# Experts' stages of a four-layer transformer block: four batches in turn in scores, merges and the way back

## The chip, the cores and the metric

The kernel runs on one core of a Trainium2 chip. Its time is device microseconds of one execution. Three runs of the kernel before took 3591.03 to 3611.88 us, median 3601.45 us.

## The reference

The input x is 8 batches of 1024 tokens of 256 numbers, fp32. Four layers are added to it, each on a layer norm without weights: a banded attention, experts, a dense attention, and the same experts again. The change touches the experts alone:

```python
def _L0_ffn_ref(x, gate_w, gate_b, w1, w2):          # x is the layer norm; E = 32 experts, K = 8
    logits = jnp.einsum('bsd,ed->bse', x, gate_w) + gate_b
    probs = jax.nn.softmax(logits, axis=-2)           # over the tokens of a batch
    vals_t, idx_t = jax.lax.top_k(probs.transpose(0, 2, 1), K)   # each expert takes 8 tokens
    tok = jnp.take_along_axis(x, flat_idx[:, :, None], axis=1).reshape(b, K, E, d)
    merged = jnp.einsum('bked,bke->bed', tok, vals)   # their weighted sum
    h = jnp.einsum('bei,eih->beh', jnp.concatenate([merged, ones], -1), w1)
    h = jax.nn.gelu(h, approximate=False)
    o = jnp.einsum('bej,ejo->beo', jnp.concatenate([h, ones], -1), w2)
    out_tok = jnp.einsum('beo,bke->bkeo', o, vals)    # the same weights on the way back
    return jnp.zeros_like(x).at[jnp.arange(b)[:, None], flat_idx].add(out_tok)
...
x = x + _L0_attn_a_ref(_layernorm(x), ...)
x = x + _L0_ffn_ref(_layernorm(x, axis=-1), L0_ffn_gate_w, L0_ffn_gate_b, L0_ffn_w1, L0_ffn_w2)
x = x + _L0_attn_b_ref(_layernorm(x), ...)
x = x + _L0_ffn_ref(_layernorm(x, axis=-1), L0_ffn_gate_w, L0_ffn_gate_b, L0_ffn_w1, L0_ffn_w2)
```

## The kernel before

x stays on the chip as x_sb: 64 tiles of 128 tokens by 256 numbers, tile t being tokens 128·(t mod 8) of batch t div 8. The function ffn is called twice, as f1 and f2; both are called f_ in the profile. PSUM is taken as eight banks of 128 x 512 numbers, all under the name f_ps. Each engine runs its own list in the order in which the code writes it, and semaphores tie the lists together; no planner sets an order in this function. It has four parts.

Setup (from L1521) makes mean and 1/deviation of each tile, turns biases and gate weights, and starts to load the weights of the first four experts.

The block "choose" has three stages. In the **scores**, VectorE normalises a tile into one of four buffers (z_tile, L1654), TensorE turns it (L1593), ScalarE takes four turned tiles, a chunk, to zT (L1631), TensorE multiplies the chunk by the gate weights (logit, L1582) and VectorE adds the gate's bias (L1661). A chunk is half a batch: 512 tokens of one batch, whose 32 scores land in the 32 PSUM partitions of that batch, 32·(b mod 4). The scores of four batches stand above one another in logits, in two such groups gq. In the **choice**, for each group, VectorE finds the eight largest of a row (L1677), marks them (L1683), ScalarE makes exponentials and their sum (L1637), VectorE sets all but the marked ones to zero and divides (L1687, L1690); TensorE turns these weights wT (L1604) and ScalarE copies them to wtok (L1642). In the **merges**, the tiles are normalised anew, even ones by VectorE, odd ones by ScalarE (L1648), and TensorE sums each batch's tiles with its weights, L1615, batch after batch, into 32 partitions of a bank. The sums are copied and turned (L1697, L1621, L1702).

The block "run" first goes through the experts in groups of four (from L1781): this **loop** isn't changed. The **way back** closes it: the experts' outputs are fetched as o_batch, again four batches above one another, and for each tile TensorE multiplies a batch's 32 rows of weights by its 32 rows of outputs (L1838), two tiles to a bank, banks 6 and 7 in turn; VectorE adds the bank to x_sb (L1893). In the first experts' stage it also makes the next layer norm's statistics of each tile (L1898). In the second, each batch of eight tiles is stored when it is done, one transfer of 1 MB (L1763).

An fp32 product is two passes over the array: the trace has two MATMUL records for each matmul of the code, and one for each transpose. In rows of the profile, "128*32 128x512" is 128 rows and 32 columns of the array, and 512 columns passed through it.

## Time and profile before

| what | value |
|---|---|
| median of three runs | 3601.45 us |
| profiled execution: its time | 3609.01 us |
| profiled execution: its span | 3607.2 us |
| TensorE busy | 2978.2 us, 83% |
| VectorE busy | 1693.9 us, 47% |
| ScalarE busy | 1422.5 us, 39% |
| GpSimd busy | 756.1 us, 21% |
| mean granted clock of TensorE | 0.907 |

The two experts' stages stand at 1451 to 1777 us and at 3277 us to the end. In a table of stretches, a row has the stretch's limits and length; then, with the number of instructions in brackets, the busy time of TensorE's passes (PE), its weight loads (PEld), VectorE (DVE), ScalarE (ACT) and GpSimd (POOL); then the granted clock of TensorE as a share of 2.4 GHz, the DMA's busy share, and GB/s. A timeline's row has the start, the length from first start to last end, engine, line, operation, output and inputs, and count; in square brackets how long the engine was idle before it, and what it waited for. A pass's record covers its way through the array as well, so that passes that start 0.43 us apart are 0.59 us long; what counts for a stream of them is the distance of the starts.

### The profile page before, as it was taken

What the parts mean: (1) busy time and instruction counts of PE and PEld (TensorE: products, weight loads), DVE (VectorE), ACT (ScalarE), POOL (GpSimd) and SP (SyncE); (2) the same over time, 40 slices, a digit from 0 to 9 for tenths busy, and PEclk for the clock granted to TensorE, in tenths of its full rate; (3) what the DMA queues carried; (4) which work ended last, traced back from release to release, by engine and by line L of the source; (5) the groups of instructions that cost most, each with busy time, mean ns of one, the idle gap of its engine ahead of it and who ended that gap; (6) DMA issues with size and microseconds to landing.
All of it is one profiled execution on the core that took longest, in us unless ns stands there. A gap on an engine that the chain in (4) does not pass through costs nothing. (4 is left out here: it accounts for less than half of the span.)

```text
span 3607.2 us, 100410 instructions
## 1 busy us (share of the span) xinstructions
PE 2978.2 (83%) x45340; PEld 1688.5 (47%) x45340; DVE 1693.9 (47%) x2811; ACT 1422.5 (39%) x1390; POOL 756.1 (21%) x523
## 2 busy tenths in 40 slices
PE   0488888878788886799668999998989898997898
PEld 0255555555556565344434444444444444443345
DVE  5143444334443343610646566666665666665202
ACT  0245444444544442320015445454554555563300
POOL 0334334333433331000022111111111111110000
PEclk9788898889889887899569999999999999999896
DMA  5333333233423331269132222222222222212494
GB/s 137 83 77 89 79 88 99 60 93 78 103 75 78 82 90 26 97 273 382 15 88 54 54 54 54 54 54 54 54 54 54 54 54 54 54 19 97 167 422 163
DMA packets 233159, 344.17 MB, mean 95 GB/s; under 512 B 113306, under 2 KB 141796, under 8 KB 216356
## 3 DMA queue, kind: packets, MB, share of 16 engines
q1 hardware_dynamic: 207508, 310.01, 29.5%
q10 hardware_dynamic: 25232, 27.83, 3.3%
q8 instruction: 354, 5.80, 0.7%
q14 instruction: 65, 0.53, 0.1%
HBM read 266.15 MB, written 69.24 MB: 93 GB/s over the span
## 5 line engine op out<-in xcount | busy, mean ns | idle before, releaser
L1403 DVE TENSOR_REDUCE b_tops<-b_slot 128x8 f32<-128x1024 f32 x576 | 680.1, 1219 | 361.1 <-PE b_slot L1260 181.4
L1440 ACT ACTIVATE b_probs<-b_slot 128x1024 f32<-128x1024 f32 x576 | 583.0, 1023 | 551.4 <-PE b_slot L1260 394.7
L502 POOL COPY a_q_far<-a_q_near 96x1024 bf16<-96x1024 bf16 x128 | 259.0, 2054 | 346.1 <-PE a_slot L581 215.9
L1280 PE MATMUL b_outT_ps<-b_probs,b_v 128*17 128x128 f32 (+3 forms) x4608 | 318.0, 384 | 6.2 <-ACT b_probs L1440 5.6
L1260 PE MATMUL b_slot<-b_q_stack,b_k_stack 99*128 99x512 bf16 (+3 forms) x1280 | 274.8, 321 | 43.5 <-DVE b_tops L1403 32.8
L1207 POOL TENSOR_SCALAR_AFFINE_SELECT b_probs<-b_probs 128x1024 f32<-128x1024 f32 x128 | 139.8, 1093 | 809.1 <-ACT b_probs L1440 809.1
L870 ACT ACTIVATE a_k_far<-a_k_near 96x1024 bf16<-96x1024 bf16 x128 | 258.0, 2067 | 91.1 <-DMA a_k_near<-parts_near_dram 82.5
L1260 PE MATMUL b_slot<-b_k_stack,b_q_stack 96*128 96x512 bf16 (+3 forms) x1280 | 266.7, 323 | 29.4 <-DVE b_tops L1403 20.6
L771 DVE TENSOR_TENSOR a_probs<-a_slot,a_bias_k 128x1024 f32<-128x1024 f32 x128 | 154.1, 1217 | 188.8 <-PE a_slot L581 188.3
L780 DVE TENSOR_REDUCE a_tops<-a_slot 128x16 f32<-128x1024 f32 x128 | 156.4, 1222 | 127.4 <-PE a_slot L581 126.5
L833 ACT ACTIVATE a_probs<-a_probs 128x1024 f32<-128x1024 f32 x128 | 133.2, 1053 | 182.9 <-DVE a_probs L771 167.1
L1260 PEld LDWEIGHTS b_slot<-b_q_stack,b_k_stack 99*128 99x128 bf16 x1280 | 107.0, 99 | 204.1 <-DVE b_tops L1403 61.8
L1814 PE MATMUL f_ps<-f_w_ring,f_hidT 128*32 128x256 f32 x1024 | 184.0, 380 | 2.1 <-ACT f_hidT L1855 2.1
L1260 PEld LDWEIGHTS b_slot<-b_k_stack,b_q_stack 96*128 96x128 bf16 x1280 | 97.5, 98 | 185.4 <-DVE b_tops L1403 61.5
L621 PE MATMUL a_slot<-a_bias_q,a_ident 128*128 128x512 bf16 x256 | 102.6, 492 | 96.5 <-POOL a_q_far L502 32.9
L657 PEld LDWEIGHTS a_outT_ps<-a_probs,a_v_near 128*17 128x17 f32 x8448 | 129.6, 103 | 87.4 <-issue 76.9
L657 PE MATMUL a_outT_ps<-a_probs,a_v_near 128*17 128x64 f32 (+1 forms) x8448 | 154.5, 228 | 18.5 <-issue 13.2
L1793 PE MATMUL f_ps<-f_w_ring,f_lhs 128*32 128x512 f32 x512 | 149.8, 613 | 8.0 <-POOL f_lhs L1777 8.0
L589 PE MATMUL a_slot<-a_zT,a_wqk 128*128 128x512 f32 x256 | 147.1, 682 | 3.6 <-issue 2.1
L1880 DVE TENSOR_TENSOR f_pre<-f_ps,f_b1T 128x128 f32<-128x128 f32 x32 | 7.8, 286 | 302.9 <-PE f_ps L1802 302.9
L1280 PEld LDWEIGHTS b_outT_ps<-b_probs,b_v 128*17 128x17 f32 x4608 | 96.2, 96 | 113.2 <-issue 68.5
L799 DVE TENSOR_SCALAR a_zb<-a_slot,a_bqk 128x1024 f32<-128x1024 f32 x32 | 41.1, 1284 | 224.0 <-PE a_slot L589 183.4
(217 smaller groups left out, 4515.7 us busy)
## 6 DMA issues: line engine op xcount, KB each, us to landing
f_w_ring<-in_L_ffn_w_dram SPq DMA_DIRECT2D x128, 1024.0 KB, 9.2
parts_near_dram<-a_parts ACTq DMA_DIRECT2D x96, 256.0 KB
parts_dram<-b_parts SPq DMA_DIRECT2D x96, 256.0 KB
a_k_near<-parts_near_dram SPq DMA_DIRECT2D x128, 128.0 KB, 3.0
b_k_stack<-parts_dram SPq DMA_DIRECT2D x64, 256.0 KB, 6.8
a_q_near<-parts_near_dram SPq DMA_DIRECT2D x64, 192.0 KB, 2.9
b_q_stack<-parts_dram SPq DMA_DIRECT2D x32, 384.0 KB, 4.5
values_dram<-a_v_stage SPq DMA_DIRECT2D x16, 544.0 KB, 4.6
```

What stands on the lines that cost most here:

```text
L502: pool.tensor_copy(q_far[far][0:QK_ROWS, h, :].rearrange("p (r a) -> p r a", r=LINKS), q_near[near][0:QK_ROWS, h, :].rearrange("p (a r) -> ...
L589: return pe.matmul(dst[:, c * 512:(c + 1) * 512], wqk[:, "qk".index(kind), kd, 8 * part:8 * part + 8, :].rearrange("p h d -> p (h d)"), zT ...
L657: ins = pe.matmul(outT_ps[BLK * h:BLK * h + HD + 1, lo:top], v_near[:, c, blk % 4, (HD + 1) * h:(HD + 1) * (h + 1)], probs[h][:, at:at + t ...
L771: ins = dve.tensor_tensor(probs[h][:, :].rearrange("p (k t c) -> p k t c", k=2, c=64), src[:, :].rearrange("p (k t c) -> p k t c", k=2, c=64),
L780: ins = dve.tensor_reduce(tops[:, h, :, :].rearrange("p k t -> p (k t)"), src[:, :].rearrange("p (t c) -> p t c", c=64), AX.X, ALU.max)
L870: act.activation(k_far[far][0:QK_ROWS, h, :].rearrange("p (r a) -> p r a", r=LINKS), k_near[near][0:QK_ROWS, h, :].rearrange("p (a r) -> p ...
L1260: ins = pe.matmul(dst[:, at:at + top - lo], own[0:rows, head, P * tile:P * tile + P], other[0:rows, head, lo:top], start=True, stop=True)
L1280: ins = pe.matmul(outT_ps[32 * h:32 * h + HD + 1, first:last], v1[b % 2][:, j, HG * g + h, :], src[:, base + first:base + last], start=u = ...
L1403: ins = dve.tensor_reduce(out, src, AX.X, ALU.max)
L1440: act.activation(probs_of(b, g, u, h)[:, :], slot_of(step)[:, :], ACT.Exp).then_inc(taken_act, 1)
L1793: ins = pe.matmul(bank[n][32 * j:32 * j + 32, :], lhs1[half][:, kd, j, :], w1_ring[:, j, kd, n * 512:(n + 1) * 512], start=kd == 0, stop=k ...
L1814: ins = pe.matmul(bank[4 + half][32 * j:32 * j + 32, 0:D], hidT[half][:, c, j, :], w2_ring[:, j, c, :], start=c == 0, stop=c == HE // P - 1)
```

## The change

Tiles of four batches take turns. The function tile_at(n) gives the tile that is n-th: n mod 4 is the batch in its group, and i = (n div 4) mod 8 its place in the batch. So a chunk is now tile i of each of four batches. Four chunks fill a bank of 512 tokens for four batches.

- Scores: zb has eight buffers in place of four. logit(c) has eight products of 32x128, for kd in 2, q in 4, in place of two of 32x512. VectorE adds the bias once in four chunks, to all 128 rows. The choice of the first group is written into the scores, behind VectorE's tiles of chunks 10, 11 and 12; its exponential into ScalarE's list after chunk 11; the turned weights after the last chunk's transposes.
- Merges: tile n goes to the PSUM rows of batch q = n mod 4, bank gq. The second group's choice stands between VectorE's tiles after n = 6, 12 and 18, its exponential behind ScalarE's tile 11, its turned weights ahead of tile 32.
- Way back: a unit is two tiles of each of four batches. Eight units; 16 products in the order q = 0, 1, 2, 3 for the first tile, then for the second, each batch into a bank of its own, eight banks for two units. VectorE adds banks 0 and 1 to x_sb; ScalarE copies banks 2 and 3 to the buffer spare, and GpSimd adds spare to x_sb. VectorE makes the statistics of its own four tiles of a unit, then those of GpSimd's four of the unit before.
- Output: after each unit SP issues four transfers of two tiles (256 KB) in place of one of 1 MB for each batch.
- Some semaphores between instructions of one engine or across blocks go, with no instruction added or taken away.

The core of the diff:

```diff
-            zb = ssb("zb", [P, 4, D])
+            zb = ssb("zb", [P, 8, D])
+            def tile_at(n):
+                c, q = divmod(n, 4)
+                return (4 * (c // NT) + q) * NT + c % NT
...
                     def logit(c):
-                        b, half = c // 2, c % 2
+                        gq, i = divmod(c, NT)
                         pe.wait_ge(zT_ready, c + 1)
-                        if c >= 2:
-                            pe.wait_ge(logits_ready, c - 1)
+                        if c >= 8 and c % 4 == 0:
+                            pe.wait_ge(logits_ready, c // 4 - 1)
                         for kd in range(KD):
-                            ins = pe.matmul(bank[2 + c % 2][32 * (b % 4):32 * (b % 4) + NE, :], gate_wT[:, kd, :],
-                                            zT[:, c % 2, kd, :], start=kd == 0, stop=kd == KD - 1)
+                            for q in range(4):
+                                ins = pe.matmul(bank[2 + c // 4 % 2][32 * q:32 * q + NE, i % 4 * P:(i % 4 + 1) * P], gate_wT[:, kd, :],
+                                                zT[:, c % 2, kd, q * P:(q + 1) * P], start=kd == 0, stop=kd == KD - 1)
...
+                    for n in range(B * NT):
+                        c, q = divmod(n, 4)
+                        gq, i = divmod(c, NT)
+                        if n == 0:
+                            pe.wait_ge(wtok_ready, 2)
+                        if n == B * NT // 2:
+                            turn_weights(1)
+                            pe.wait_ge(wtok_ready, 4)
...
+                        pe.matmul(bank[gq][32 * q:32 * q + NE, 0:D], wtok[:, i, gq, 32 * q:32 * q + NE],
+                                  zb[:, n % 8, :], start=i == 0, stop=i == NT - 1).then_inc(merge_done, 1)
...
 ScalarE
+                    for n in range(1, B * NT, 2):
+                        if n < 8:
+                            act.wait_ge(z_turned, B * NT)
+                        else:
+                            act.wait_ge(merge_done, n - 7)
...
+                        if n == 11:
+                            exponentials(1)
+                        if n == B * NT // 2 - 1:
+                            take_weights(1)
...
 way back, TensorE
-                    for t2 in range(B * NT // 2):
-                        if t2 >= 2:
-                            pe.wait_ge(summed, t2 - 1)
+                    for u in range(UNITS_OUT):
+                        gq, i2 = divmod(u, NT // 2)
                         for ii in range(2):
-                            b, i = (2 * t2 + ii) // NT, (2 * t2 + ii) % NT
-                            rows = slice(32 * (b % 4), 32 * (b % 4) + NE)
-                            ins = pe.matmul(bank[6 + t2 % 2][:, ii * D:(ii + 1) * D], wT[rows, b // 4, i * P:(i + 1) * P],
-                                            o_batch[rows, b // 4, :], start=True, stop=True)
-                        ins.then_inc(scattered, 1)
+                            i = 2 * i2 + ii
+                            for q in range(4):
+                                if u >= 2 and not ii:
+                                    if q < 2:
+                                        pe.wait_ge(summed, 2 * u - 3 + q)
+                                    else:
+                                        pe.wait_ge(taken, 2 * u - 5 + q)
+                                rows = slice(32 * q, 32 * q + NE)
+                                ins = pe.matmul(bank[u % 2 * 4 + q][:, ii * D:(ii + 1) * D], wT[rows, gq, i * P:(i + 1) * P],
+                                                o_batch[rows, gq, :], start=True, stop=True)
+                                if ii:
+                                    ins.then_inc(scattered, 1)
...
 way back, GpSimd, ScalarE, SP
+                    for u in range(UNITS_OUT):
+                        for q in range(2, 4):
+                            pool.wait_ge(taken, 2 * u + q - 1)
+                            xt = two_tiles(u, q)
+                            pool.tensor_tensor(xt, spare[:, q - 2, :], xt, ALU.add).then_inc(added, 1)
...
+                            act.wait_ge(scattered, 4 * u + q + 1)
+                            if u:
+                                act.wait_ge(added, 2 * u - 3 + q)
+                            act.activation(spare[:, q - 2, :], bank[u % 2 * 4 + q][:, :], ACT.Copy).then_inc(taken, 1)
...
+                            sp.wait_ge(summed, 2 * u + 2)
+                            sp.wait_ge(added, 2 * u + 2)
...
+                                sp.dma_start(out[b, i * P:(i + 2) * P, :].rearrange("(i p) d -> p i d", p=P), x_sb[:, t:t + 2, :]).then_inc(stored, 16)
```

Three places show what the change does to the lists. The first is TensorE from the end of the scores to the end of the merges, before and after; f_zb are the normalised tiles, f_zT the turned chunk, f_wT the chosen weights.

```order
-L1582 MATMUL f_ps<-f_zT,f_gate_wT 32x512 x4
-L1604 MATMUL f_ps<-ident,f_wT 128x128 x16
-L1615 MATMUL f_ps<-f_zb,f_wtok 32x256 x64
-L1621 MATMUL f_ps<-ident,f_merged 128x128 x4
```

```order
+L1599 MATMUL f_ps<-ident,f_wT 128x128 x8
+L1590 MATMUL f_ps<-f_zT,f_gate_wT 32x128 x8
+L1629 MATMUL f_ps<-f_zb,f_wtok 32x256 x32
+L1599 MATMUL f_ps<-ident,f_wT 128x128 x8
+L1629 MATMUL f_ps<-f_zb,f_wtok 32x256 x32
+L1634 MATMUL f_ps<-ident,f_merged 128x128 x4
```

The weights of the first group are turned ahead of the last scores, and those of the second half way through the merges. The second place is VectorE from the last chunks of the scores into the merges, after the change; before, the steps MAX to the division, of both groups, stood together between the last scores and the first tile of the merges.

```order
+L1679 TENSOR_SCALAR f_zb<-x_sb,f_mv,f_rstd 128x256 x4
+L1690 MAX f_top<-f_logits 128x8
+L1692 TENSOR_SCALAR f_neg_max<-f_top 128x1
+L1679 TENSOR_SCALAR f_zb<-x_sb,f_mv,f_rstd 128x256 x4
+L1698 MATCH_REPLACE f_marked<-f_top,f_logits 128x1024
+L1679 TENSOR_SCALAR f_zb<-x_sb,f_mv,f_rstd 128x256 x4
+L1703 RECIPROCAL f_inv<-f_total 128x1
+L1704 SCALAR_TENSOR_TENSOR f_wT<-f_marked,f_wT 128x1024
+L1707 TENSOR_SCALAR f_wT<-f_wT,f_inv 128x1024
+L1679 TENSOR_SCALAR f_zb<-x_sb,f_mv,f_rstd 128x256 x4
+L1685 TENSOR_SCALAR f_logits<-f_ps,f_gate_b 128x512
```

Each step of the choice is followed by four tiles. The third is VectorE in the first way back, before and after.

```order
-L1893 TENSOR_TENSOR x_sb<-f_ps,x_sb 128x512
-L1898 BN_STATS stats<-x_sb 128x6 x2
-L1893 TENSOR_TENSOR x_sb<-f_ps,x_sb 128x512
-L1898 BN_STATS stats<-x_sb 128x6 x2
-L1893 TENSOR_TENSOR x_sb<-f_ps,x_sb 128x512
-L1898 BN_STATS stats<-x_sb 128x6 x2
```

```order
+L1976 TENSOR_TENSOR x_sb<-f_ps,x_sb 128x512 x2
+L1981 BN_STATS stats<-x_sb 128x6 x4
+L1967 BN_STATS stats<-x_sb 128x6 x4
+L1976 TENSOR_TENSOR x_sb<-f_ps,x_sb 128x512 x2
+L1981 BN_STATS stats<-x_sb 128x6 x4
+L1967 BN_STATS stats<-x_sb 128x6 x4
```

Sixteen sums of 512 numbers leave VectorE's list and stand in GpSimd's; the 64 statistics stay.

## Rows read from the trace of the kernel before

**Rows 1.** Stretches: first stage (scores, choice, merges, loop, way back), second's end

```profile
1460.20:1508.70 48.50, 47.09 (x192) 21.07 (x192) 34.10 (x81) 18.87 (x33) 0.00 (x0) 0.96 0.36 149
1508.70:1520.90 12.20, 3.94 (x16) 3.13 (x16) 9.78 (x16) 4.65 (x9) 0.00 (x0) 0.63 0.00 0
1520.90:1548.10 27.20, 27.14 (x128) 12.32 (x128) 12.37 (x30) 18.23 (x32) 0.00 (x0) 0.92 0.00 1
...
1550.60:1723.90 173.30, 161.88 (x832) 73.19 (x832) 4.63 (x18) 16.37 (x33) 4.25 (x12) 0.97 0.85 342
1723.90:1776.60 52.70, 51.05 (x128) 38.55 (x128) 45.52 (x97) 0.00 (x0) 0.00 (x0) 0.50 0.00 0
...
3550.50:3602.30 51.80, 51.06 (x128) 38.57 (x128) 22.10 (x32) 0.00 (x0) 0.00 (x0) 0.50 0.42 142
3602.30:3607.20 4.90, 0.00 (x0) 0.00 (x0) 0.02 (x1) 0.00 (x0) 0.00 (x0) 0.50 0.63 214
```

**Rows 2.** Timeline of one chunk of the first scores

```profile
1500.40 1.09 PE L1593 MATMUL f_ps<-ident,f_zb 128*128 128x128 f32 x8
1500.51 0.75 DVE L1661 TENSOR_SCALAR f_logits<-f_ps,f_gate_b 32x512 f32<-32x512 f32 x1 [0.70 <-PE f_ps L1582]
1501.15 1.09 ACT L1631 ACTIVATE f_zT<-f_ps 128x512 f32<-128x512 f32 x2 [1.77 <-PE f_ps L1593]
1501.29 1.38 DVE L1654 TENSOR_SCALAR f_zb<-x_sb,f_mv,f_rstd 128x256 f32<-128x256 f32 x4
...
1501.42 1.90 PE L1582 MATMUL f_ps<-f_zT,f_gate_wT 128*32 128x512 f32 x4
...
1503.26 1.09 PE L1593 MATMUL f_ps<-ident,f_zb 128*128 128x128 f32 x8
```

**Rows 3.** Timeline, second attention: products to four column groups

```profile
2308.44 0.41 PE L1280 MATMUL b_outT_ps<-b_probs,b_v 128*17 128x128 f32 x8
...
2321.44 1.38 PE L1280 MATMUL b_outT_ps<-b_probs,b_v 128*17 128x512 f32 x12
```

**Rows 4.** Timeline of the first stage: the exponential, ScalarE's tiles in the merges

```profile
1510.18 1.15 ACT L1637 ACTIVATE f_wT<-f_logits,f_neg_max 128x1024 f32<-128x1024 f32 x1 [3.79 <-DVE f_neg_max L1679]
...
1520.79 1.08 ACT L1648 ACTIVATE f_zb<-x_sb,f_shift,f_rstd 128x256 f32<-128x256 f32 x2
...
1522.90 0.60 ACT L1648 ACTIVATE f_zb<-x_sb,f_shift,f_rstd 128x256 f32<-128x256 f32 x1 [1.02 <-PE f_ps L1615]
```

**Rows 5.** Stretches at the start of the first scores

```profile
1460.80:1464.20 3.40, 3.39 (x16) 3.24 (x16) 3.33 (x10) 1.73 (x3) 0.00 (x0) 0.52 1.00 424
1464.20:1467.10 2.90, 2.90 (x14) 1.22 (x12) 1.53 (x4) 0.90 (x3) 0.00 (x0) 1.00 1.02 429
```

**Rows 6.** Timelines of the first way back, and of statistics before it

```profile
1730.11 1.05 PE L1838 MATMUL f_ps<-f_o_batch,f_wT 32*128 32x256 f32 x3
...
1731.26 1.05 PE L1838 MATMUL f_ps<-f_o_batch,f_wT 32*128 32x256 f32 x2
...
1730.11 0.41 PEld L1838 LDWEIGHTS f_ps<-f_o_batch,f_wT 32*128 32x128 f32 x2
...
1734.06 0.69 DVE L1893 TENSOR_TENSOR x_sb<-f_ps,x_sb 128x512 f32<-128x512 f32 x1
...
1447.97 2.70 DVE L762 BATCH_NORM_STATS2 stats<-x_sb 128x6 f32<-128x256 f32 x8
```

**Rows 7.** Lines of GpSimd's sums, and timeline of one beside VectorE

```profile
L476 POOL TENSOR_TENSOR a_spread<-a_tops,a_among x32: 664/667/676, 168.9 to 1385.5; 128x256 f32<-128x256 f32 x32
...
L488 POOL TENSOR_TENSOR a_zb<-a_zb,a_parts x32: 2119/2126/2134, 106.4 to 1292.3; 128x1024 f32<-128x1024 f32 x32
...
1298.47 4.03 POOL L494 TENSOR_TENSOR a_parts<-a_zb,a_parts 128x1024 bf16<-128x1024 f32 x1 [4.00 <-ACT a_parts L859]
...
1298.21 2.29 DVE L756 SCALAR_TENSOR_TENSOR a_flat<-a_gate,a_flat 128x2048 f32<-128x2048 f32 x1
```

**Rows 8.** A stretch inside one output transfer

```profile
3559.50:3562.00 2.50, 2.50 (x7) 2.00 (x6) 0.79 (x2) 0.00 (x0) 0.00 (x0) 0.50 1.02 348
```

218 lines of the change are left out of this document (125 added, 93 removed).

## The prediction

> **What bounds the kernel now.** I read the table of stages first, then the timeline of one step inside each stage, then the chain of waits of the last stage, and last the rows that price what the trace of before doesn't have. The two experts' stages are the only ones the change touches. In the first, scores run from 1460.2 to 1508.7, the top-8 choice to 1520.9, merges to 1548.1; then the experts' loop to 1723.9 and the way back to 1776.6 [rows 1]. The second repeats this within 0.5 us a stage (its way back, 3550.5 to 3602.3, and 4.9 us of output DMA after it are shown). The loop isn't touched: TensorE is busy in 161.88 of its 173.30 us, the DMA at 342 GB/s, and its first weights were loaded in the scores (149 GB/s over 48.5 us). So 173 us stay in each experts' stage, and what can move is 48.5 + 12.2 + 27.2 + 52.7 us in the first and the like in the second.
>
> In scores and merges TensorE is busy nearly all the time (47.09 of 48.50, 27.14 of 27.20) but each product uses 32 of the array's 128 columns. One chunk of four tiles takes 2.86 us: 1.02 us from the start of its eight transposes to the scores, 1.84 us for the scores, while VectorE works 1.38 + 0.75 us and ScalarE 1.09 us [rows 2]. In the way back each product uses 32 rows of 128, and the granted clock is 0.50, that is 1.2 GHz [rows 1].
>
> **Scores.** A chunk is now one tile of each of four batches. An fp32 product is two passes, so before it is 4 passes of 512 columns, 0.43 us apart; now it is 16 passes of 128, a quarter as long, 0.107 us, to four column groups in turn. That groups run beside each other is seen in the second attention: 8 passes of 128 columns to four groups take 0.41 us in all, where eight in series start over 0.86, and 12 of 512 columns take 1.38 us, in series 5.1 [rows 3]. So four rounds of 0.107 = 0.43, plus the 0.13 that the scores took beyond their four passes (1.84 - 1.71): 0.56, and TensorE needs 1.58 us a chunk. In series it would need 1.84 + 1.02 again: that is the other end.
>
> VectorE is then as late. Four tiles in 1.38 with 0.41 for one are 0.32 apart: 64 x 0.32 = 20.7. The bias add of four batches is one instruction of 0.75 in four chunks: 3 x 0.75 = 2.2 inside the loop. The first group's top-8 steps move into the loop: both groups together cost VectorE 9.78 us, less two tiles 8.96, so 4.5 for one. Some fifteen restarts after waits at 0.1 each make 1.5. Sum 28.9, against 16 x 1.58 + 1 (the turned weights) = 26.3 for TensorE; with eight z buffers either can be a chunk ahead, so the larger counts, not the sum. The exponential on ScalarE (1.15 us, [rows 4], and the table it loads) fits into its slack of 16 x (1.8 - 1.09). Behind the last tile stand half a transpose chunk, the turned weights, the last scores and their bias add: about 2.9. Scores: 32 instead of 48.5 us, **-16.5** (bounds: -18.5 with perfect overlap of VectorE and TensorE, 0 in series).
>
> **Top-8.** The 12.2 us in which TensorE works 3.94 go from the path: the first group's steps are in the 28.9, the second's stand between the tiles of the first merges. **-12.2** (bounds -12.2 and -7.7, if the 4.5 of the second group add to the merges).
>
> **Merges.** Before, two passes of 256 columns a tile set the pace. Now four tiles in turn go to four groups, and the next is the normalised tile itself. ScalarE makes every second one, two in 1.08 with 0.60 for one [rows 4], so 0.48 apart: 32 x 0.48 = 15.4. Into its queue come the exponential, 1.15 (all tiles behind it wait, which TensorE feels after the buffers are used up), and after tile 31 the second group's weights: TensorE turns 8 blocks, the 1.02 that eight transposes take in the scores, or double at half clock, and ScalarE copies twice: 2.3. Sum 18.9. VectorE needs 32 x 0.32 + 4.5 + hand-overs = 16, within it. 27.2 becomes 19.2: **-8** (bounds -10 and 0). For the couplings between the three engines, whose waits no row shows, I give back 2.7 in each stage: **-34** for scores to merges, -68 for both.
>
> **Way back.** 64 tiles, 128 passes of 32x256. Before all passes that follow each other are in one row group, 0.427 us apart at 1.2 GHz; only where the batch changes they overlap: three passes in 1.05 us there, two in 1.05 elsewhere, and the weight loads of two groups stand within 0.41 [rows 6]. Now four groups take turns, eight tiles a unit: 16 passes, four rounds, 1.7 us if they overlap fully, 6.8 in series. Weight loads of 128 columns come along; they overlapped at the batch change too, so I take 1.7 to 2.6. What else a unit needs: VectorE two adds, 0.69 each; ScalarE two copies, the 0.49 apart that two take in the scores (1.09 for two, [rows 2]); GpSimd two adds of 512 elements, between its 0.667 for 256 and 2.126 for 1024 [rows 7]; on the line between them 1.15, so 2.3. GpSimd's pace could suffer from VectorE: one of its adds took 4.03 us instead of 2.13 beside VectorE's operation on two SBUF inputs, 2.29 us long [rows 7]. VectorE's adds here have one input in PSUM, and its statistics one input in all, so I take no such loss; its price would be 1.4 a unit at most.
>
> First stage: VectorE also makes the statistics of eight tiles, eight in 2.70 [rows 6]; a unit is 1.4 + 2.7 + 0.1 = 4.2, longer than all others. 8 x 4.2 = 33.9, plus 2.1 until the first unit is there and 0.4 at the end: 36.4 instead of 52.7, **-16.3**. Before it was 32 x (0.69 + 0.75) = 46 of VectorE's time in the same stage, with waits; that the statistics run in blocks saves the rest.
>
> Last stage: no statistics, so the output DMA is next: eight units of 1 MB. Within a transfer the DMA moves 348 GB/s [rows 8], 3.0 us a unit, more than GpSimd's 2.3. First data after 2.1 (products) + 0.6 + 1.15 + 1.15 (copy, two adds) + 1.0 ahead of the transfer; then 24.1, and 0.9 to the end (before, 4.9 us pass from the last add to the end, of which the last 1 MB is 3.0, so 1.9 stand around it): 31.1 from the start of the way back, against 51.8 + 4.9 = 56.7: **-25.6** (bounds: -28 without any lead, 0 with row groups in series, since 8 x 6.8 = 54.4).
>
> **Sum.** -68 - 16.3 - 25.6 = -110 us. The profiled execution has a span of 3607.2 and a time of 3609.0, 0.2% over the median of the runs, 3601.45. From that median: 3491.5, so 3492.
>
> **The rivals.** *Half clock in the scores.* With the scores short, TensorE is mostly transposing, and the clock may stay at 1.2 GHz: transposes 1.7, scores 0.85 and 0.3 of hand-overs are 2.9 a chunk, no better than now. It costs 16 us a stage, 3524. Against it: in the first 3.4 us of this stage TensorE did nothing but transposes, at 0.52, and right behind the clock was 1.00 [rows 5]; and merges on a quarter of the columns are at 0.92 [rows 1]. For it: the way back stays at 0.50 with 51.05 us busy, so a busy record alone doesn't raise the clock, and the new stage leaves gaps. The Trainium skill ("TensorE: Matmul & The Clock Gate", Part 4: PE-mode transpose) says that transposes don't count as busy for the clock. By that rule this rival would be likely; the row on the 3.4 us speaks against it here.
>
> *The way back stays in series.* Weight loads of 128 columns, not the passes, set 3.4 us a unit or more, up to 6.8: the last stage gives 0 to -22, the first 0 to -16; in the middle 3512. Against it the overlap at the batch change.
>
> *The packing costs instead.* In the scores there are four times as many passes and weight loads, each pass only 0.107 long. If a load can't hide behind a pass of another column group (0.11 each, exposed), the chunk is 16 x 0.217 + 1.02 = 4.5 us: +26 a stage. If row groups behave alike, the way back gains nothing. With top-8's -12.2 and merges at 0 that is +28, 3630, slower than before. It decides where an exposed load makes the chunk longer than 2.86, so from 0.01 us a load on. The Trainium skill (the same page, Part 3: Packing small matmuls) says that loads overlap running matmuls only when the row group differs, and that matmuls start in program order. By the first half this rival would hold; the 8 passes in 0.41 us, loads included, say otherwise for column groups.
>
> **How the numbers follow.** Forecast 0.75, half clock 0.14, way back in series 0.06, packing costs 0.03, and 0.02 for a wait that I haven't seen and that leaves little. Own range of the forecast 3475 to 3510: couplings 0 to 8 a stage, a unit of 3.9 to 4.6, merges 17 to 22. To hold eight in ten with half clock in it: 3474 to 3530. Faster by over 0.5% (18 us, what a measurement tells from none) holds in the first three: 0.95; within 0.5% 0.02; slower 0.03.
>
> **What would show it.** Scores of about 32 us with chunks of 1.8; the granted clock in them near 1.00; no gap between scores and merges; merges of 19 us with ScalarE busy throughout; way back of 36 us with VectorE as the only busy engine, and one of 31 us to the end with the DMA full from its sixth us on. A clock of 0.50 in the scores, passes of scores over 0.11 us apart in one chunk, or GpSimd adds over 1.5 us would prove steps wrong.

## The result, and the profile after

Four runs of the kernel after took 3475.52 to 3491.6 us, median 3486.51; four of the kernel before, median 3597.19. The ratio is 0.9682 with a 95% interval of 0.9644 to 0.9721: 111 us less. The forecast was 3492, range 3474 to 3530.

In the profiled execution (3486.47 us, span 3484.7) the stretches that answer to [rows 1] are, from the table of stretches: scores, merges, loop and way back of the first experts' stage, then the second way back to the end.

```profile
1449.40:1485.80 36.40, 31.19 (x392) 23.27 (x392) 28.56 (x77) 22.14 (x39) 0.00 (x0) 0.89 0.47 197
1485.80:1506.60 20.80, 16.72 (x136) 6.06 (x136) 15.81 (x40) 17.39 (x35) 0.00 (x0) 1.00 0.00 1
1509.10:1680.50 171.40, 160.13 (x832) 72.60 (x832) 4.67 (x18) 16.36 (x33) 4.23 (x12) 0.99 0.85 346
1680.50:1713.40 32.90, 17.95 (x128) 12.66 (x128) 30.55 (x80) 9.12 (x16) 19.74 (x16) 0.55 0.00 1
3451.90:3484.70 32.80, 16.34 (x128) 11.05 (x128) 10.35 (x17) 9.44 (x16) 19.62 (x16) 0.60 0.77 257
```

There is no stretch for the choice any more. The granted clock in the scores is 0.89 and in the merges 1.00, and the way back has GpSimd busy.

To compare kernels I take four spans in each trace: in both experts' stages from VectorE's first normalised tile to the end of the last merge, and from the way back's first product to the stage's end. In this table "scores" ends with the last product of the scores, "gap" is the time from there to the first merge. All in us.

| kernel | scores | gap | merges | first tile to end of merges, 1st / 2nd stage | way back 1st / 2nd | sum of the four |
|---|---|---|---|---|---|---|
| before | 47.6 | 13.0 | 27.1 | 87.7 / 87.5 | 52.6 / 56.6 | 284.4 |
| after | 35.4 | 1.3 | 20.3 | 57.0 / 56.1 | 32.7 / 32.7 | 178.5 |
| way back only | 48.0 | 13.1 | 27.4 | 88.4 / 87.9 | 32.7 / 32.5 | 241.5 |
| scores only | 36.9 | 1.3 | 20.3 | 58.5 / 56.2 | 52.6 / 56.6 | 223.9 |
| choice apart | 29.0 | 14.1 | 16.3 | 59.4 / 59.6 | 32.7 / 32.5 | 184.2 |
| groups one by one | 35.1 | 1.3 | 20.3 | 56.8 / 56.7 | 32.7 / 32.4 | 178.6 |
| no GpSimd | 35.5 | 1.3 | 20.3 | 57.1 / 56.3 | 42.2 / 31.4 | 187.0 |
| four buffers | 35.1 | 1.3 | 25.5 | 61.8 / 61.7 | 32.7 / 32.2 | 188.4 |
| choice spread | 32.4 | 1.3 | 20.0 | 53.7 / 53.8 | 32.7 / 32.2 | 172.4 |
| GpSimd tiles | 31.4 | 1.3 | 21.6 | 54.3 / 53.7 | 32.7 / 32.1 | 172.8 |
| combined | 31.5 | 1.3 | 21.2 | 54.0 / 54.1 | 32.7 / 29.5 | 170.3 |
| combined, merges only | 31.9 | 1.3 | 21.4 | 54.6 / 54.5 | 32.7 / 29.5 | 171.3 |
| two units by group | 35.5 | 1.3 | 20.3 | 57.1 / 56.8 | 35.4 / 40.1 | 189.4 |
| last version | 30.9 | 1.3 | 20.0 | 52.2 / 52.3 | 32.7 / 29.5 | 166.7 |

The four spans became 284.4 - 178.5 = 105.9 us shorter. The rest of the program, which no kernel here touches, took 3607.2 - 284.4 = 3322.8 us in the profile of before and 3306.2 in that of after; in the other twelve it lies between 3302.3 and 3320.2. So a whole time carries some 10 us of chance either way, and effects below that are read from these spans. The spans have some chance too: the first scores of five kernels that run them with the same choice and buffers (after, scores only, groups one by one, no GpSimd, two units by group) take 35.1 to 36.9 us, the second ones 34.5 to 35.2.

The timeline of one undisturbed chunk of the scores, to set beside [rows 2]:

```profile
1457.65 1.09 PE L1609 MATMUL f_ps<-ident,f_zb 128*128 128x128 f32 x8
1458.41 1.08 ACT L1655 ACTIVATE f_zT<-f_ps 128x512 f32<-128x512 f32 x2 [0.51 <-PE f_ps L1609]
...
1458.67 0.65 PE L1590 MATMUL f_ps<-f_zT,f_gate_wT 128*32 128x128 f32 x16
...
1459.25 1.09 PE L1609 MATMUL f_ps<-ident,f_zb 128*128 128x128 f32 x8
```

1459.25 - 1457.65 = 1.60 us a chunk instead of 2.86: the same transposes, and sixteen passes in 0.65 where four took 1.90. The same timeline where the first group's choice stands:

```profile
1472.01 1.41 PE L1609 MATMUL f_ps<-ident,f_zb 128*128 128x128 f32 x8 [0.50 <-DVE f_zb L1679]
...
1474.15 0.16 DVE L1703 RECIPROCAL f_inv<-f_total 128x1 f32<-128x1 f32 x1 [1.23 <-ACT f_wT L1641]
...
1476.61 1.41 PE L1609 MATMUL f_ps<-ident,f_zb 128*128 128x128 f32 x8 [2.61 <-DVE f_zb L1679]
...
1478.86 1.97 PE L1609 MATMUL f_ps<-ident,f_zb 128*128 128x128 f32 x8
```

VectorE waits 1.23 us for the exponential and only then goes on to three more steps of the choice; TensorE, whose next tile comes behind them, stands still for 2.61 us. Behind that gap eight transposes take 1.97 us instead of 1.09: half clock, until about 1481.

The second experts' stage has the same gap, and the clock stays full behind it. First the transposes there, then a stretch behind the gap in the first and in the second stage:

```profile
3247.74 1.41 PE L1609 MATMUL f_ps<-ident,f_zb 128*128 128x128 f32 x8 [2.61 <-DVE f_zb L1679]
...
3249.69 1.41 PE L1609 MATMUL f_ps<-ident,f_zb 128*128 128x128 f32 x8
```

```profile
1478.10:1481.50 3.40, 3.40 (x40) 2.54 (x32) 2.66 (x9) 1.74 (x3) 0.00 (x0) 0.50 0.02 5
3247.70:3254.90 7.20, 7.13 (x96) 4.83 (x96) 4.20 (x12) 4.46 (x9) 0.00 (x0) 1.00 0.01 3
```

The two chunks behind the gap start 2.25 and 2.81 us behind the ones before them in the first stage, 1.95 and 1.92 in the second: the half clock costs 1.2 us where it comes, the gap comes in both. Twelve stages of the kernels here have this gap, and in ten of them half clock follows. At the start of the scores the clock is at half until 4.6 and 5.3 us behind the first tile here, 3.7 and 3.4 in the kernel before, 3.2 to 6.6 in all; most of the chance in the scores comes from these two places.

The way back, one unit of the first stage:

```profile
1696.26 1.08 ACT L1947 ACTIVATE f_spare<-f_ps 128x512 f32<-128x512 f32 x2 [2.32 <-PE f_ps L1906]
1696.59 1.27 DVE L1976 TENSOR_TENSOR x_sb<-f_ps,x_sb 128x512 f32<-128x512 f32 x2
1696.94 2.49 POOL L1841 TENSOR_TENSOR x_sb<-f_spare,x_sb 128x512 f32<-128x512 f32 x2 [1.24 <-ACT f_spare L1947]
...
1697.32 2.68 PE L1906 MATMUL f_ps<-f_o_batch,f_wT 32*128 32x256 f32 x16 [1.12 <-DVE x_sb L1976]
1697.78 1.40 DVE L1981 BATCH_NORM_STATS2 stats<-x_sb 128x6 f32<-128x256 f32 x4
1699.09 1.39 DVE L1967 BATCH_NORM_STATS2 stats<-x_sb 128x6 f32<-128x256 f32 x4
1700.07 1.09 ACT L1947 ACTIVATE f_spare<-f_ps 128x512 f32<-128x512 f32 x2 [2.72 <-PE f_ps L1906]
1700.40 1.27 DVE L1976 TENSOR_TENSOR x_sb<-f_ps,x_sb 128x512 f32<-128x512 f32 x2
```

VectorE has no gap, the other three do: a unit is 1700.40 - 1696.59 = 3.81 us. GpSimd's add beside it stays at 1.25 us, with none of the loss seen in [rows 7]. In the second way back the end of the chain of waits (start, length, engine, what, line, count) and the queue of output transfers read:

```profile
3451.99 2.21 PE f_ps L1906 x16
3454.20 0.58 ACT f_spare L1947
3454.86 18.40 POOL x_sb L1841 x15
```

```profile
3457.45 24.43 SPq L1820 DMA_DIRECT2D out_dram<-x_sb  x32
```

The first transfer is issued 5.46 us behind the first product, since SP waits for both of GpSimd's adds. From then on the DMA is full, 342 GB/s in 3470 to 3475, but for one hole between the first unit and the second:

```profile
3457.45 3.60 SPq L1820 DMA_DIRECT2D out_dram<-x_sb  x4
```

```profile
3460.00:3462.00 2.00, 1.38 (x16) 0.94 (x16) 0.84 (x3) 1.10 (x2) 2.00 (x2) 1.00 0.61 201
```

In these 2 us the DMA's share is 0.61 instead of 1.0, which is 0.8 us lost. GpSimd isn't the cause: its adds for the second unit end 7.82 us behind the first product, but SP spends 3.60 us on issuing the first four transfers and comes to the fifth only at 9.16. Why the third and fourth take SP 0.99 and 1.60 us, against 0.40 and 0.46 for the first two, no run shows. The output ends at 3484.7.

### The profile page after: what moved, and what is told of

Its sections match the earlier page's. It is cut to its first block and busy times, and to the rows that moved or that the text cites. A ratio compares the mean times of both kernels' runs of the same rounds, so it can differ in the third digit from the quotient of the medians.

```text
span 3484.7 us, 101224 instructions
## 1 busy us (share of the span) xinstructions
PE 2844.4 (82%) x45724; PEld 1622.0 (47%) x45724; DVE 1644.5 (47%) x2755; ACT 1435.7 (41%) x1422; POOL 794.2 (23%) x555
## 5 line engine op out<-in xcount | busy, mean ns | idle before, releaser
L1260 PE MATMUL b_slot<-b_k_stack,b_q_stack 96*128 96x512 bf16 (+3 forms) x1280 | 265.7, 322 | 29.5 <-DVE b_tops L1403 20.8
L657 PE MATMUL a_outT_ps<-a_probs,a_v_near 128*17 128x64 f32 (+1 forms) x8448 | 152.8, 227 | 19.2 <-issue 15.3
```

Of the source, the lines that this page charges most:

```text
L657: ins = pe.matmul(outT_ps[BLK * h:BLK * h + HD + 1, lo:top], v_near[:, c, blk % 4, (HD + 1) * h:(HD + 1) * (h + 1)], probs[h][:, at:at + t ...
L1260: ins = pe.matmul(dst[:, at:at + top - lo], own[0:rows, head, P * tile:P * tile + P], other[0:rows, head, lo:top], start=True, stop=True)
```

## The experiments

**Each half alone.** One kernel has the scores, choice and merges of before with the way back of after; the other the reverse.

```diff
 way back only                          scores only
-    the block "choose" of after        -    the block "run" of after
+    the block "choose" of before       +    the block "run" of before
```

> The scores, the choice and the merges are those of the kernel before; the way back, the spare buffer and the output in units are those of the kernel after. Theory (the two halves of the change don't touch each other): from the first normalised tile to the end of the merges 87.9 us in both experts' stages, as before; way back 32.8 us in the first stage and 32.7 us to the end in the second, as after. Sum 19.9 + 24.0 = 44 us less than before, ratio 0.988. Rival 1 (the way back's gain depends on the new order ahead of it, for instance through the clock): the first way back over 36 us. Rival 2 (part of the 110 us came from elsewhere, as the stretch ahead of the first experts' stage was 10.8 us shorter in the profile after): this kernel and the one with the scores alone then save together less than 100 us.

> The scores, the choice and the merges are those of the kernel after; the way back and the output are those of the kernel before (passes of one batch after the other, VectorE adds all, 1 MB transfers). Theory: first tile to the end of the merges 57.0 us as after, 30.9 less than before in each stage; way back 52.7 us and 56.7 us to the end as before. Sum 62 us less than before, ratio 0.983. Together with the way back alone: 106 us, ratio 0.971 if nothing is coupled. Rival: scores and merges at full clock need the later order; then this saves under 50 us.

Measured: 3558.93 us (four runs, 3555.99 to 3572.35), ratio 0.9879 (0.9850 to 0.9909), and 3538.92 us (four runs, 3530.47 to 3541.59), ratio 0.9807 (0.9783 to 0.9832). The product of both is 0.9688, against 0.9682 for both halves together; the four spans save 42.9 and 60.5 us, together 103.4 against 105.9. Each half keeps its own times, as the table shows, but for the first scores of scores only, 36.9 us against 35.4, where the clock is at half for 6.3 us at the start and for longer behind the gap. So the halves are independent within some 2 us. The two together save more than the 100 us of rival 2, and the four spans hold 105.9 of the 111 us; what is left is within the chance of whole times.

**Groups one by one.** The prediction says that four groups overlap because they take turns in the code. Here they don't take turns.

```diff
-                        for kd in range(KD):
-                            for q in range(4):
+                        for q in range(4):
+                            for kd in range(KD):
...
-                        for ii in range(2):
-                            for q in range(4):
+                        for q in range(4):
+                            for ii in range(2):
```

> The kernel after, with the same products written in another order: all passes of one batch (one column group in the scores, one row group in the way back), then all of the next; four passes of a group stand behind one another. The merges are as in the kernel after. Theory A (passes start in the order of the code; one waits until the pass before it in its own group has gone through, and the next group's first pass goes along with the last of the group before): the scores of a chunk need 13 steps of 0.107 instead of 4, 1.4 us instead of about 0.55, so a chunk 2.4 us instead of 1.60 and the scores some 12 us longer (48 instead of 36); the way back 13 steps of 0.427 = 5.5 us a unit, more than VectorE's 3.8, so 45 us in both stages instead of 32.8 and 32.7. Sum about +50 us. Rival B (TensorE lets a later group's pass overtake one that waits): all as after, within 2 us a stage. Rival C (the clock rises to 1.00 in the way back because TensorE is then busy throughout): passes 0.213 apart, units of 2.8 us, way back unchanged, only the scores longer.

Measured: 3496.85 us (four runs, 3486.36 to 3501.74), ratio 0.9701 (0.9679 to 0.9724), the four spans 178.6 us against 178.5; the 10 us more of the whole time are not in them. Rival B holds, theory A falls. The stretch of 1.90 us from the way back's first product, first of the kernel after, then of this one:

```profile
1680.50:1682.40 1.90, 1.85 (x16) 1.57 (x20) 0.00 (x0) 0.00 (x0) 0.00 (x0) 0.50 0.05 9
```

```profile
1676.70:1678.60 1.90, 1.86 (x16) 1.63 (x17) 0.00 (x0) 0.00 (x0) 0.00 (x0) 0.50 0.03 9
```

Sixteen passes start in it either way. In order of the code, with four of a group behind one another 0.427 apart and the next group beginning beside the last, six could have at most. So passes of a later group go ahead of waiting ones. The kernel after needs this too, if less of it, since a product is two passes of one group. A chunk's sixteen passes take 0.66 us here, and rival C, the clock, is out as well: it is 0.50 in both rows and 0.55 over the whole first way back of both kernels.

**How far this goes.** Now eight passes of each group stand in a row, for two units at once.

```diff
+                    for w in range(UNITS_OUT // 2):
+                        for q in range(4):
+                            for u in 2 * w, 2 * w + 1:
...
+                                for ii in range(2):
...
+                                    ins = pe.matmul(bank[u % 2 * 4 + q][:, ii * D:(ii + 1) * D], ...
```

> The kernel after, but in the way back the products of two units are written group by group: 8 passes of one row group in a row, then 8 of the next; all eight banks are filled from 32 passes. Theory (TensorE lets a later group's pass overtake waiting ones over at least a dozen places in the list, as the version with four in a row showed): the last group's first pass, 25th in the list, starts within 0.1 us of the first, and the first way back stays within 1 us of 32.7. Rival (it looks ahead 16 passes or fewer): the third or fourth group starts 0.43 us or more later, the first unit's last bank is ready later by 0.9 to 2.6 us, and the way back takes 33.5 to 36 us.

Measured: 3502.84 us (two runs), ratio 0.9727 (0.9703 to 0.9751); the way back takes 35.4 and 40.1 us. The theory falls; the rival is right that there is a limit, though not in its number. The first two stretches of 1.90 us, and the whole first way back:

```profile
1685.10:1687.00 1.90, 1.82 (x4) 1.50 (x5) 0.03 (x1) 0.00 (x0) 0.00 (x0) 0.50 0.03 9
1687.00:1688.90 1.90, 1.90 (x9) 1.69 (x8) 0.69 (x1) 0.00 (x0) 0.00 (x0) 0.50 0.00 0
```

```profile
1685.10:1720.60 35.50, 31.88 (x128) 27.75 (x128) 30.96 (x81) 9.12 (x16) 19.91 (x16) 0.50 0.00 1
```

Four passes start in the first stretch and eight in the second (the nine counted there include one that is still running): at first one group runs, then two. In the trace's records the second group's first pass, ninth in the list, starts together with the first group's fifth, 1.87 us behind the start, while the sixth to eighth are still to come. That is what a place for four passes of a group, the running one among them, would give: the fifth of a group blocks the list until the first has gone.

With two of a group in a row (the kernel after) or four, all groups run; with eight, two do, and the 33rd pass of the list starts 7.5 us behind the first instead of 3.6. In the second way back the first transfer is issued only at 9.76 us, and pairs of units come 7.5 us apart, more than the 6 us that the DMA needs for two: 40.1. The reading is inferred from these three kernels; rows of three, five or six were not tried.

The Trainium skill ("TensorE: Matmul & The Clock Gate", Part 3: Packing small matmuls) says that matmuls start and end strictly in program order, with a window of reordering for weight loads only. The last two experiments contradict it on the starts: of different row groups, with the sixteen starts in 1.90 us where program order allows six, and of column groups, with the 0.66 us for sixteen passes where it would take some 1.4 by theory A.

**Choice apart.** Packing stays, the choice goes back between scores and merges.

```diff
-                        if c == 10:
-                            top_max(0)
-                        if c == 11:
-                            top_mark(0)
-                        if c == 12:
-                            top_weights(0)
                     logits_of(3)
+                    for gq in range(2):
+                        top_max(gq)
+                        top_mark(gq)
+                        top_weights(gq)
...
```

> The kernel after, but both groups' choice stands between scores and merges, as in the kernel before; packing of four batches, eight z buffers and the new way back stay. Theory (the choice written into the scores costs them almost 5 us, by gaps and by half clock behind one of them): scores 31.5 us instead of 36.2, then about 12.2 us of choice, merges 16.5 to 17.5 instead of 20.3; sum 61 us from the first tile to the end of the merges instead of 57.0, +4 us a stage, +8 us in all. Rival 1 (the forecast of the prediction: the choice fits in for nothing but VectorE's own time): scores 32 less 4.5 of VectorE's steps = 27.5, which the TensorE bound of 1.60 us a chunk lifts to 29, so 59 in all. Rival 2 (hiding the choice gave all 12.2 us): scores stay at 36, +12 us a stage.

Measured: 3502.81 us (four runs, 3487.61 to 3507.26), ratio 0.9700 (0.9669 to 0.9732). Scores, choice and merges of the first stage:

```profile
1463.80:1492.90 29.10, 28.28 (x384) 22.08 (x384) 23.46 (x68) 18.27 (x33) 0.00 (x0) 0.89 0.60 249
1492.90:1507.00 14.10, 3.96 (x19) 3.13 (x16) 11.09 (x19) 5.39 (x10) 0.00 (x0) 0.67 0.00 0
1507.00:1523.30 16.30, 16.26 (x128) 5.13 (x128) 11.38 (x28) 15.71 (x32) 0.00 (x0) 0.87 0.00 1
```

Taking the choice out makes the scores 6.4 us and the merges 4.0 us shorter and adds 12.8 of gap: 2.4 us more in the first stage, 3.5 in the second. So of the 30.7 us between first tile and merges packing brings 28.3, and hiding the choice only the last 2.4. Merges without it are 32 of ScalarE's tiles at 0.4975: 15.9, and 0.4.

The sum of 59.4 to 59.6 is rival 1's 59 and not the theory's 61. But rival 1 also has the choice cost the scores no more than VectorE's own 4.5 us, and it costs them 6.4 and 5.4; there the theory is right. The clock at the start of these scores is at half for 6.4 and 6.6 us, longer than in the kernel after, so that 2.4 and 3.5 rather overstate what hiding the choice brings.

**Choice spread.** The same steps, further apart.

```diff
-                        if c == 11:
+                        if c == 10:
                             exponentials(0)
...
                         if c == 12:
-                            top_weights(0)
+                            top_zero(0)
+                        if c == 14:
+                            top_scale(0)
```

> The kernel after, with the steps of the choice further apart: the exponential one chunk earlier in ScalarE's list; VectorE's reciprocal and zeroing behind chunk 12 and its last scaling behind chunk 14 (in the second group behind tiles 18 and 22), so that it waits for no step of its own and not for the exponential. Theory (the 6.4 us that the choice costs the scores are 1.23 us of waiting, a gap of TensorE of 2.6 us and the half clock behind that gap): no gap above 1 us and no half clock, scores 33 us instead of 36.2, merges 20 as before, -3 to -4 us a stage. Rival (the choice costs VectorE's own 4.5 us, which the buffers cannot hide since VectorE has only 0.2 us of slack a chunk): scores 35.5 to 36, no gain beyond the 1.23.

Measured: 3480.61 us (four runs, 3479.25 to 3487.48), ratio 0.9670 (0.9644 to 0.9697); scores 32.4 instead of 35.4, in the second stage 32.6 instead of 34.5, merges 0.3 shorter. The stretch of the scores, and the chunk where the gap of 2.61 was:

```profile
1454.70:1487.20 32.50, 30.32 (x392) 22.05 (x392) 27.55 (x75) 21.38 (x38) 0.00 (x0) 0.93 0.53 222
```

```profile
1477.21 1.41 PE L1609 MATMUL f_ps<-ident,f_zb 128*128 128x128 f32 x8 [0.51 <-DVE f_zb L1679]
...
1479.70 1.41 PE L1609 MATMUL f_ps<-ident,f_zb 128*128 128x128 f32 x8 [0.50 <-DVE f_zb L1679]
```

No gap is over 0.62 us, and no transposes behind the start of the scores take 1.97. The chunks of the choice are 2.49 us apart here, VectorE's own pace with four tiles and a step in each, and that is what is left: 3.4 us over the scores of the kernel without the choice. The theory is right on the first stage (-3.3 us) and falls short on the second (-2.3 for -3 to -4), where there was no half clock to take away. The rest is what the rival names. By my estimate it is even nearer to its 4.5 us: the first three chunks of the kernel without the choice take 0.8 us longer, by half clock until 6.4 us instead of 4.6, so that at the same clock the rest would be 4.2.

**Four buffers.**

```diff
-            zb = ssb("zb", [P, 8, D])
+            zb = ssb("zb", [P, 4, D])
```

> The kernel after with four z buffers instead of eight, in scores and merges. Theory (the buffers let VectorE run a chunk ahead of TensorE, which hides hand-overs and part of the choice): undisturbed chunks of 1.9 us instead of 1.60, the stall behind the choice longer by a chunk, so scores 42 us instead of 36; merges 22 instead of 20.3; sum +7 us a stage. Rival (VectorE and TensorE already wait on one another in each chunk, buffers don't matter): within 1 us a stage.

Measured: 3499.78 us (two runs), ratio 0.9725 (0.9690 to 0.9760). Neither expectation holds: the scores don't notice (35.1 against 35.4 us, 35.0 against 34.5), the merges take 25.5 us instead of 20.3. Both engines' tiles there now wait for buffers; ScalarE's queue shows it:

```profile
1502.39 1.09 ACT L1668 ACTIVATE f_zb<-x_sb,f_shift,f_rstd 128x256 f32<-128x256 f32 x2 [0.22 <-PE f_ps L1629]
1503.71 1.09 ACT L1668 ACTIVATE f_zb<-x_sb,f_shift,f_rstd 128x256 f32<-128x256 f32 x2 [0.22 <-PE f_ps L1629]
```

Two tiles every 1.32 us instead of 1.00. So eight buffers are worth 5 us a stage, all of it in the merges. The prediction's argument for them, that in the scores either engine can be a chunk ahead, bought nothing: there four do as well.

**No GpSimd in the way back.**

```diff
-                        for q in range(2):
+                        for q in range(4):
                             dve.wait_ge(scattered, 4 * u + q + 1)
...
-                            act.activation(spare[:, q - 2, :], bank[u % 2 * 4 + q][:, :], ACT.Copy).then_inc(taken, 1)
...
-                            pool.tensor_tensor(xt, spare[:, q - 2, :], xt, ALU.add).then_inc(added, 1)
```

> The kernel after, but in the way back VectorE adds all four banks of a unit from PSUM; ScalarE copies nothing and GpSimd adds nothing. Theory (VectorE is the bound of the first way back, the output DMA that of the second): VectorE's unit of 3.81 us grows by two adds of 0.64, to 5.1, so the first way back takes 8 x 5.1 + 2.2 = 43 us instead of 32.7; in the second four adds are 2.6 us a unit, below the 3.0 of the DMA, so 32 to 33 us to the end as now. Sum +10 us. Rival (GpSimd's adds of 2.45 us a unit and the hand-over through ScalarE set the pace in the second way back): it gets shorter by more than 1.5 us without them, 31 us or less.

Measured: 3498.94 us (two runs), ratio 0.9722 (0.9688 to 0.9757).

```profile
1684.80:1727.00 42.20, 24.80 (x128) 17.55 (x128) 40.11 (x96) 0.00 (x0) 0.00 (x0) 0.54 0.00 0
3466.60:3498.00 31.40, 17.72 (x128) 13.76 (x128) 19.23 (x32) 0.00 (x0) 0.00 (x0) 0.61 0.80 268
```

First stage 42.2 us (expected 43): GpSimd is worth 9.5 us there, so of the 19.9 saved about half is its work. Of the other 10.4 us, 5.0 are waits of VectorE for products behind the first one, of which this kernel has none, and 5.4 are VectorE's own: the same 32 adds and 64 statistics, in blocks, take it 40.1 us instead of 45.5. The second stage takes 31.4 us, 1.3 less than with GpSimd. The theory's 32 to 33 falls, and so does the rival's 31 or less, though it has the direction right. GpSimd doesn't set the pace there. 0.8 of the 1.3 is that the first transfer is issued 4.7 us behind the first product instead of 5.46, and the rest that the DMA has less of a hole behind it, 25.1 us from first to last packet instead of 25.6.

**GpSimd makes tiles.** On top of the choice spread, GpSimd normalises every fourth tile of the scores and a quarter of those of the merges.

```diff
+            MAKERS = "DAPDAPDA"
...
+                    for n in range(3, B * NT, 4):
+                        if n >= 8:
+                            pool.wait_ge(z_turned, n - 7)
+                        z_tile(n)
...
+                        pool.tensor_scalar(zb[:, n % 8, :], x_sb[:, t, :], mv[:, t, 0:1], rstd[:, t:t + 1], ...
```

> The spread choice, and GpSimd, which is idle there, normalises every fourth tile of the scores and a quarter of those of the merges (VectorE 3, ScalarE 3, GpSimd 2 of eight). Theory (VectorE is the late engine in the scores, ScalarE in the merges): VectorE has then 0.5 us of slack a chunk, so the choice is hidden and TensorE's 1.60 us a chunk sets 29.5 us; merges go by ScalarE's 24 tiles of 0.50 and 3.4 us of exponential and weights, 15.5 us; from first tile to the end of the merges 47 us instead of 57. Rival (GpSimd is slow beside VectorE, as in the row of 4.03 us against 2.13 before, or its own tile takes over 1.6 us): the chunk is GpSimd's, scores 36 us or more, merges 20 or more, no gain.

Measured: 3483.65 us (four runs, 3478.74 to 3494.24), ratio 0.9690 (0.9658 to 0.9722). Scores 31.4 and 30.8, merges 21.6: against the choice spread 1.0 and 1.8 us less, and 1.6 more. The theory's 47 us from the first tile to the end of the merges falls (54.3 and 53.7), and the rival is right on the merges alone. GpSimd is simply full there: it makes two of eight tiles, back to back at 1.24 us, 2.49 us for eight. From GpSimd's queue in the merges of the next experiment, where it makes every eighth tile:

```profile
1499.94 1.38 POOL L1596 TENSOR_SCALAR f_zb<-x_sb,f_mv,f_rstd 128x256 f32<-128x256 f32 x1 [0.78 <-PE f_ps L1658]
1502.09 1.22 POOL L1596 TENSOR_SCALAR f_zb<-x_sb,f_mv,f_rstd 128x256 f32<-128x256 f32 x1 [0.78 <-PE f_ps L1658]
```

A tile takes GpSimd 1.22 to 1.38 us, and then it waits 0.78 for its buffer, which is always the same one of eight: 2.15 us for eight tiles, longer than 8 x 0.249 = 1.99 that VectorE and ScalarE need. TensorE merges in the order of the tiles, so by this reading the slowest maker sets the pace even with one tile of eight; the last version tests it.

**Versions put together.** The second way back also changes: VectorE adds all banks, and SP waits for each bank alone. The three expectations are, in this order, those of the rows "combined", "combined, merges only" and "last version" of the table.

```diff
-                            sp.wait_ge(summed, 2 * u + 2)
-                            sp.wait_ge(added, 2 * u + 2)
                             for q in range(4):
+                                if q < 2:
+                                    sp.wait_ge(summed, 2 * u + q + 1)
+                                else:
+                                    sp.wait_ge(added, 2 * u + q - 1)
```

> A version put together from what the runs showed: the choice spread; GpSimd normalises every fourth tile of the scores but only every eighth of the merges (VectorE four, ScalarE three of eight), since its tile took 1.24 us there; in the second way back VectorE adds all four banks, ScalarE and GpSimd none, and SP waits for one bank at a time before its transfer of 256 KB. Theory: scores 31 us; merges by ScalarE's 24 tiles of 0.50, the exponential and the weights, 15.5 to 17 us; 49 to 50 us from first tile to the end of the merges instead of 57; first way back 32.7 as before; in the second the first transfer is issued 2.8 us behind the first product's start, instead of 5.46, and the DMA is full from there on: 29 to 30 us to the end instead of 32.7. Sum 17 us less than the kernel after, about 3470 us. Rival (smaller waits of SP in the second way back leave the DMA with gaps, or issuing is the bound): 31 us or more there; and merges at 20 us if the order of the makers, not their number, sets their pace.

> As the combined version, but VectorE normalises all tiles of the scores, GpSimd none there. Theory (GpSimd's tile of 1.3 us just fits into a chunk of 1.60, so it takes the choice's time off VectorE): scores 32.5 us here against 31.3, all else alike, +2.4 us in all against the combined version. Rival (GpSimd delays as much as it takes over): scores the same or shorter here.

> The combined version with merges made by VectorE and ScalarE alone, every second tile each, as in the kernel after; GpSimd still normalises every fourth tile of the scores; the second way back as in the combined version. Theory (in the merges a GpSimd tile holds up the ring of eight buffers: its 1.24 us and 0.78 us until the merge of its buffer is seen and the hand-over to TensorE make 2.15 us for eight tiles, more than eight tiles of the two other engines take, 1.99): merges 20.0 us instead of 21.2, first tile to the end of the merges 52.7 us, 1.3 less a stage than the combined version and 4 less than the kernel after; second way back 29.5. Sum 11 us less than the kernel after, 3475 us. Rival (the first 32 tiles' choice, not GpSimd, made the 21.2): merges 21 or more again.

Measured: 3479.91 us (five runs, 3478.27 to 3486.25), ratio 0.9666 (0.9648 to 0.9684); 3487.51 us (five runs, 3477.86 to 3503.59), ratio 0.9692 (0.9665 to 0.9719); and 3485.93 us (six runs, 3470.97 to 3493.10), ratio 0.9681 (0.9658 to 0.9705). The second way back takes 29.5 us in all three, as expected, with the first transfer issued 2.8 us behind the first product in the first of them. The merges of the first two were missed by some 4 us and are 20.0 in the last version without GpSimd's tiles, as expected, so its tile did cost the 1.2 us. The first pair of scores has GpSimd gain only 0.4 to 0.5 us there, where 1.2 was expected, but their clocks differ at the start. Between stages with like clock it gains 1.0: 31.5 us (combined, half clock until 4.8 us) against 32.4 and 32.6 (choice spread, 4.6 and 4.9), and 30.9 and 31.1 (last version, 3.8) against 31.9 and 32.0 (combined, merges only, 3.5 and 3.6). So the theory holds nearly in size, and the rival falls. Scores, merges and both ways back of the last version:

```profile
1444.50:1475.50 31.00, 29.47 (x392) 21.84 (x392) 24.34 (x59) 20.94 (x38) 22.53 (x16) 0.94 0.56 232
1475.50:1496.80 21.30, 16.79 (x136) 5.87 (x136) 16.55 (x41) 18.21 (x37) 0.00 (x0) 1.00 0.00 1
1671.20:1703.90 32.70, 17.95 (x128) 12.62 (x128) 30.55 (x80) 9.12 (x16) 19.75 (x16) 0.55 0.00 1
3439.40:3469.00 29.60, 17.73 (x128) 13.75 (x128) 19.23 (x33) 0.00 (x0) 0.00 (x0) 0.62 0.86 284
```

Its four spans are 11.8 us shorter than those of the kernel after, as expected (11). Its whole time isn't shown to be: 3485.93 against 3486.51, and the intervals of the ratios are 8 to 14 us wide on each side. The spans are shorter in one profile, of the fastest of its six runs; a gain of the whole over the kernel after is not proved by these runs. The same holds for the choice spread, GpSimd's tiles and the other two versions.

## Why the prediction was right, and where it was not

The sum was right: 110 us were forecast, 105.9 are in the four spans, 111 between the medians. What bounds the merges and both ways back was right too. That the sum came so near is in part luck: scores to merges gave 6 us less than forecast in both stages together, the first way back 3.6 more and the second 1.7 less, and the last 5 us between the spans and the medians are within chance. The terms:

- **Scores, -16.5 forecast.** The chunk was right, 1.60 us against 1.58. The stage was not: 36.2 us from the first tile to the last score instead of 32. The step that failed is that "either can be a chunk ahead, so the larger counts, not the sum". VectorE's total includes a choice that stands in three chunks, and the slack it has in the other thirteen doesn't help there. To the last score's bias add, as the forecast counts, it takes 29.8 us without the choice, where the rule gives 25.3 + 2.9 = 28.2, and 33.2 with the choice spread, where it gives 31.8. What the rule lacks in both is about the half clock at the start: their first three chunks start 2.0 and 1.2 us later than 1.60 apart would have it. What it costs that the steps stand close together, the 3.0 us from 33.2 to 36.2, is in the chunk of the gap, 4.60 us instead of 2.49, 1.23 of it the wait for the exponential, and in the half clock behind it, 1.2.
- **Choice, -12.2.** It did leave the path, but 6.4 us came back in the scores and 4.0 in the merges. The forecast had 2.6 in the scores (28.9 against 26.3) and 3.5 in the merges.
- **Merges, 19.2.** Its own terms add up to 18.9; no row gives the other 0.3. Measured 20.3. ScalarE's pace is 0.4975 us a tile for 0.48, 15.9 in all, its exponential and weights take the 3.5 forecast, and it waits 0.42 us for VectorE and once 0.97 until TensorE frees a buffer.
- **Couplings.** The 2.7 us a stage were too few: without them the forecast is -36.7, measured are -30.7 and -31.4, so 5.3 to 6.0 would have been right.
- **First way back, 36.4.** Measured 32.7. Mis-sized is the unit: 4.2 us was the sum of records' lengths, and records of VectorE overlap by some 0.1 us each; from start to start it is 3.81. 8 x 3.81 + 2.2 = 32.7. (8 x 4.2 is also 33.6, not the 33.9 written.) That VectorE is the bound was right, the experiment without GpSimd shows it.
- **Second way back, 31.1.** Measured 32.7. The first transfer was forecast 5.0 us behind the first product and came at 5.46, the DMA ran at 342 instead of 348 GB/s, 0.4 us over 8 MB, and the hole between the first two units cost 0.8. The forecast took the DMA as full from the first unit on and had no term for what SP spends on issuing. The experiments show what this lead is worth: 31.4 without GpSimd, 29.5 with a wait for each bank.
- **Half clock in the scores** did not come, though TensorE turns tiles in two thirds of its time there: the clock is at half for the first 4.6 and 5.3 us (before, 3.7 and 3.4 [rows 5]), and in the first stage for 3.4 us behind the one gap. The Trainium skill ("TensorE: Matmul & The Clock Gate", Part 4: PE-mode transpose) says that transposes don't count as busy for the clock; the trace of before, with 3.4 us of nothing but transposes at 0.52 and 1.00 right behind them, doesn't agree, and the row was the better guide.
- **In series, or packing costs:** neither. Sixteen passes in 0.65 us (0.56 forecast) exclude an exposed weight load of any size that matters. The reason that I gave, groups that take turns, isn't needed: four passes of one group may stand in a row.

## What to carry to other kernels

Products that use 32 rows or columns of the array run four at a time if they are of different groups; with four passes of one group in a row nothing was lost, with eight half of it was. When work moves into the shadow of another engine, look at the few steps where it stands, not at the stage's totals: spread it until no step waits for another engine's answer. A ring of buffers filled by several engines went at the pace of the slowest one's round trip. A store should wait for its own piece only: with that, and without GpSimd, the second way back became 3.2 us shorter. Compare stages of the scores only where the clock at their start is alike.

## What was not expected of the hardware

GpSimd takes 1.22 us and more (1.24 back to back, up to 1.8 in the scores) for one operation with two scalars per partition on 128x256 numbers, but 0.667 for an add of two tensors of that size [rows 7]. The start of passes out of the order of the code, and its limit, are told above, and so is the clock, which fell in ten of twelve stages behind the same gap of 2.6 us.
